# Moving the context's keys and values of a latent attention from the third phase of a two-layer kernel to its first, with the first phase's work put in a new order

## The chip, the cores and the metric

The kernel runs on 1 core of a Trainium2 chip. The metric is the device time of one execution in microseconds (us). A core has five engines with a queue of instructions each, worked through in order: TensorE (PE in the profile; PEld is its loading of weights), VectorE (DVE), ScalarE (ACT), GpSimd (POOL) and SyncE (SP), which here only starts DMAs. Engines wait for each other through semaphores. Matmul results land in PSUM, eight banks `Q[0]` to `Q[7]` of 128 x 512 float32.

## The reference

64 sequences of 128 tokens of width 256 go through two layers. Only what matters here is shown; `ctx_1024` is a second input, (64, 128, 256), that no step changes.

```python
x = x + L0_attn(layernorm(x), ...)            # state-space mixer: projection, convolution, decay matrices
x = x + L0_xattn(layernorm(x), ctx_1024, ctx_1024, mask, ...)   # cross attention on ctx_1024
x = x + L0_ffn(layernorm(x), ...)             # 16 experts, 2 per token, and a shared one
x = x + L1_attn(layernorm(x), ...)            # causal attention
x = x + L1_xattn(ctx_1024, layernorm(x), mask, ...)             # the latent attention
x = x + L1_ffn(layernorm(x), ...)             # ternary projection

# in L1_xattn(x=ctx_1024, latents=layernorm(x)):
x = layer_norm(x, ln_x_w, ln_x_b)             # of the context: depends on ctx_1024 alone
latents = layer_norm(latents, ln_l_w, ln_l_b)
kv = concatenate([x, latents], axis=1) @ Wkv  # 128 context rows, 128 latent rows
k, v = split(kv, 2, axis=-1)                  # 8 heads of 64
k = l2norm(k) * k_scale                       # per head: k / max(sqrt(sum k^2), eps)
```

The context's half of `k` and `v` does not depend on the stream `x`, so it can be computed at any time.

## The kernel before, in words

All 64 sequences are blocks of 128 tokens, one token on each partition. The program has three phases. Phase 1 does the mixer, the cross attention, the router and the shared expert; phase 2 the routed experts, tile by tile; phase 3 the causal attention, the latent attention and the last projection.

Phases 1 and 3 are software pipelines. The work of a block is cut into chains, and each chain into steps; a Python generator yields the name of each step and emits its instructions on one engine. In phase 1 the chains are M (first norm, time step, cumulative sums), V (projection, convolution), N (decay matrices and the mixer's output), Y (keys and values of the cross attention), X (cross attention) and F (router, shared expert). In phase 3 they are A (causal attention), C (the context's keys and values), K (latent queries, keys, values), L (latent attention) and T (output projection and ternary layer). `program(eng, engine, phase, stages)` gives each chain a lag in blocks, so that one round of the loop holds M and V of block n, N of block n-1, X of block n-2, F of block n-3. There are 64 blocks and a few rounds to fill and drain.

What stands behind what within a round is written out by hand: `ORDER[phase][engine]` is a list of tokens, the chain's letter and the step's name (`Ftop` is step `top` of chain F). `weave` walks the list. So each engine's queue is fixed, and a waiting instruction holds up all behind it. Names used below:

- `was(eng, name, b)` waits for the previous block's signal of that name, `done` for this block's.
- `Ncb0` to `Ncb3` (SP): the cumulative sums, written to memory by `Mco`, come back broadcast to all partitions, 512 KB for 8 heads each. `Nd0` to `Nd3` (POOL, L618) subtract from them, `Ng`, `Ne` (ACT, L1199, L1202) take the absolute value and the exponential, `Nm0` to `Nm2` (DVE, L847) and `Nm3` (POOL, L622) multiply by the masked product, `Nv0` to `Nv3` (PE) contract, `Ny0`, `Ny1` (DVE, L852) bring the result out, `Nyg` and `Nrms` (POOL) gate and scale it, `Npr` projects it, `Nx1` (DVE, L861) adds it to the stream.
- `Vcv` to `Vcv3` (DVE, L817 and L819): the convolution; `Vxs2` (L826) its gate; `VxsT` (PE) turns it; `Vxdt` (DVE, L836, L837) scales it; `Vz` (PE) is another projection into the same bank, so it waits for `Vxdt`; `Vtz` (ACT) and `Vgz` (DVE, L841) gate.
- `Ftop` (DVE, L893 to L905) picks two experts; `Fslot` their rows; `Fsc` (POOL, L646) scatters the rows to memory. `Mdt`, `Mab`, `Msp` make the time step; `Msp` on POOL is a chain of 13 small instructions (L594 to L610). `Xho` (DVE, L784, L785, L880) ends the cross attention with `x2`, from which the router's norm `Fln3` starts.
- Norms: moments on DVE, the root of the variance on POOL (`centre` or `rstd`), the scaling on ACT or DVE, the turn on PE, its copy on ACT.

Chain C in phase 3: load the context rows (`Cc`), norm them, turn them into `cT`, multiply by the keys' half of `Wkvl` (`Cla1`, in two halves `Cla1`, `Cla1h`), square (`Clq0` on ACT), sum per head (DVE), root (POOL, L682), scale (`Clu0`), turn (`ClT0`), copy into `klT`, then the values' half (`Cla3`, `Cla3h`) and copy into `Vl`. It uses bank `Q[3]` alone; K uses `Q[4]`. In phase 1 chain Y loads the same context rows, turns them on PE (`YcT`) and copies them (`cT` on ACT) before it multiplies.

## Time and profile before

| | |
|---|---|
| median of 3 runs | 4805.45 us (4796.27 to 4813.17) |
| the profiled execution | 4825.85 us, of it the span 4824.2 us |
| busy | PE 4196.8 us, DVE 3385.8, ACT 2902.8, POOL 2741.4 |
| phase 1 | 0 to about 2500 us |
| phase 2 | about 2500 to 2800 us |
| phase 3 | about 2800 to 4824 us |
| data moved | 304.09 MB, 63 GB/s over the span |

Read the three phases apart: PE is busy for 82% of phase 1 and for 99% of phase 3. The round of a phase is the first and the last start of an instruction that runs once a block, divided by 63.

### The profile page before, as it was taken

Reading aid. Unit: us, or ns where it says so; the run is one execution under the profiler, and the core shown is the slowest. Engines: PE = TensorE matmul, PEld = TensorE weight load, DVE = VectorE, ACT = ScalarE, POOL = GpSimd, SP = SyncE. Lnnn points to the kernel's source line nnn. Section 1 sums busy time; section 2 is a strip of 40 time slices with the busy share of each in tenths; the row PEclk is TensorE's granted clock in tenths of the full one; section 3 lists DMA queues with packets and bytes.
Section 4 is the critical chain, followed back from the end, with each engine's and each line's share of the span. In section 5 each row is a group of like instructions: output and inputs, shape, how many; then the busy total and the mean of one; then the engine's idle time right before and its main releaser. Section 6 shows DMA issues by size and latency. Waiting matters only on the chain. (4 is left out here: it accounts for less than half of the span.)

```text
span 4824.2 us, 120433 instructions
## 1 busy us (share of the span) xinstructions
PE 4196.8 (87%) x34006; PEld 3000.4 (62%) x34071; DVE 3385.8 (70%) x8668; ACT 2902.8 (60%) x7030; POOL 2741.4 (57%) x4093
## 2 busy tenths in 40 slices
PE   3888888888888888888869979999999999999998
PEld 2555555555555555555547756666666666666665
DVE  2776677666776677766745547877777777777776
ACT  2666666666666666666634436666666666666564
POOL 3666666666666666666622235555555555555554
PEclk8999999999999999999979989999999999999999
DMA  5222222222222222222214411111111111111110
GB/s 156 72 92 81 74 74 78 93 76 74 74 83 88 75 74 74 90 82 74 74 58 145 142 41 30 31 31 31 30 30 30 31 31 31 31 31 31 31 30 19
DMA packets 215885, 304.09 MB, mean 63 GB/s; under 512 B 56608, under 2 KB 167456, under 8 KB 215840
## 3 DMA queue, kind: packets, MB, share of 16 engines
q1 hardware_dynamic: 188864, 240.33, 16.2%
q0 software_dynamic: 19200, 52.45, 3.3%
q10 hardware_dynamic: 7776, 10.75, 0.7%
q8 instruction: 23, 0.38, 0.0%
q14 instruction: 22, 0.18, 0.0%
HBM read 239.19 MB, written 64.23 MB: 63 GB/s over the span
## 5 line engine op out<-in xcount | busy, mean ns | idle before, releaser
L1402 PE MATMUL Q<-ident,arena 128*128 128x128 f32 x4768 | 824.8, 298 | 141.0 <-ACT arena L1145 48.9
L1402 PEld LDWEIGHTS Q<-ident,arena 128*128 128x128 f32 x4768 | 570.3, 149 | 385.2 <-issue 135.8
L1397 PE MATMUL Q<-Wkvl,arena 128*128 128x512 f32 x1024 | 498.7, 599 | 0.0
L618 POOL TENSOR_TENSOR arena<-arena 128x1024 f32<-128x1024 f32 x256 | 479.6, 1890 | 6.7 <-DMA arena<-cum_rows 6.7
L682 POOL TENSOR_TENSOR l<-l,half_pow 128x8 f32<-128x8 f32 x192 | 318.8, 1661 | 230.4 <-DVE l L1025 228.8
L707 POOL TENSOR_TENSOR arena<-arena,part_of 128x512 f32<-128x512 f32 x256 | 264.1, 1043 | 188.6 <-DVE part_of L1063 187.7
L769 DVE TENSOR_REDUCE mx<-Q 128x4 f32<-128x512 f32 x512 | 343.8, 681 | 9.3 <-PE Q L1425 4.7
L1440 PE MATMUL Q<-arena 128*17 128x128 f32 x4096 | 243.2, 313 | 102.3 <-ACT arena L1162 102.2
L1431 PE MATMUL Q<-ident,arena 128*128 128x128 f32 x2048 | 300.0, 280 | 23.3 <-ACT arena L1162 18.4
L1431 PEld LDWEIGHTS Q<-ident,arena 128*128 128x128 f32 x2048 | 231.9, 141 | 132.3 <-issue 93.6
L1155 ACT ACTIVATE arena<-Q,mx 128x128 f32<-128x128 f32 x1024 | 282.6, 374 | 0.5 <-DVE mx L769 0.5
L1425 PE MATMUL Q<-arena 32*128 32x128 f32 x4096 | 281.9, 276 | 0.0
L1202 ACT ACTIVATE arena<-arena 128x1024 f32<-128x1024 f32 x256 | 268.6, 1049 | 0.1
L1199 ACT ACTIVATE arena<-arena 128x1024 f32<-128x1024 f32 x256 | 268.1, 1047 | 0.0
L1425 PEld LDWEIGHTS Q<-arena 32*128 32x128 f32 x4096 | 262.8, 189 | 3.2
L1361 ACT ACTIVATE arena<-Q,mxl 128x256 f32<-128x256 f32 x512 | 235.8, 473 | 46.2 <-DVE mxl L1058 38.9
L1497 PE MATMUL Q<-arena 128*16 128x128 f32 x4096 | 164.3, 278 | 107.6 <-DVE arena L847 98.1
L1440 PEld LDWEIGHTS Q<-arena 128*17 128x17 f32 x4096 | 146.4, 106 | 178.2 <-issue 163.8
L1162 ACT ACTIVATE arena<-Q 128x512 f32<-128x512 f32 x384 | 220.0, 589 | 56.6 <-PE Q L1431 55.8
L847 DVE TENSOR_TENSOR arena<-arena 128x1024 f32<-128x1024 f32 x192 | 233.2, 1242 | 2.9 <-ACT arena L1202 2.9
L1397 PEld LDWEIGHTS Q<-Wkvl,arena 128*128 128x128 f32 x1024 | 169.6, 190 | 103.8 <-issue 103.6
L819 DVE SCALAR_TENSOR_TENSOR arena<-arena,convw 128x128 f32<-128x128 f32 x768 | 225.8, 356 | 6.8
(312 smaller groups left out, 10634.8 us busy)
## 6 DMA issues: line engine op xcount, KB each, us to landing
arena<-cum_rows SPq DMA_DIRECT2D x256, 512.0 KB, 6.3
arena<-routed_rows SPq DMA_DIRECT2D x144, 128.0 KB, 2.1
expert_rows<-arena POOLq DMA_DIRECT2D x144, 128.0 KB, 2.0
arena<-in_x_dram SPq DMA_DIRECT2D x128, 128.0 KB, 5.1
arena<-in_ctx_dram SPq DMA_DIRECT2D x128, 128.0 KB
x_rows<-arena SPq DMA_DIRECT2D x128, 128.0 KB, 1.7
arena<-x_rows SPq DMA_DIRECT2D x128, 128.0 KB, 2.4
out_dram<-arena SPq DMA_DIRECT2D x64, 128.0 KB, 1.7
```

The lines of the kernel that those rows point to most:

```text
L618: tell(g.tensor_tensor(E8[j], E8[j], cums[:, 8 * j:8 * j + 8].unsqueeze(2).broadcast_to([P, 8, T]), ALU.subtract), "diff")
L682: link(pool, c, b, g.tensor_tensor(l2[:, k, :], l2[:, k, :], half_pow[:, :], ALU.pow), bare=True)
L707: tell(g.tensor_tensor(both, both, part_of[:, 2 * k:2 * k + 2].unsqueeze(2).broadcast_to([P, 2, 2 * T]), ALU.mult), "Pln")
L769: largest = v.tensor_reduce(mx[:, 4 * j:4 * j + 4], pj, AX.X, ALU.max, negate=True)
L1155: last = s_.activation(S[:, j, g, :], banks[j][:, g * T:(g + 1) * T], ACT.Exp, bias=mx[:, 4 * j + g:4 * j + g + 1])
L1199: tell(s_.activation(Ew[j], Ew[j], ACT.Abs), "gap")
L1202: tell(s_.activation(Ew[j], Ew[j], ACT.Exp, scale=-1.0), "E")
L1397: last = mm(out, lhs(c), rhs(c), start=c == 0, stop=c == n - 1)
L1402: last = nc.tensor.transpose(out[:, c * P:(c + 1) * P], src[:, c * P:(c + 1) * P], ident[:, :])
L1425: last = mm(banks[j][:, g * T:(g + 1) * T], QT[r, g, :], KT[r, g // 2, :], start=False, stop=g == NG - 1)
L1431: last = nc.tensor.transpose(bank[:, g * T:(g + 1) * T], S[:, j, g, :], ident[:, :])
L1440: last = mm(bank[32 * (h % 4):32 * (h % 4) + AW + 1, h // 4 * T:(h // 4 + 1) * T], V[:, h, :], PT[:, j, g, :], start=True, stop=True)
```

## The change

Chain C leaves phase 3 and joins phase 1 with the lag of chain X. Its keys and values are written to two new tensors in memory by a new chain S on SP one round later, and chain L of phase 3 loads them into the places where C had put them. C in phase 1 has two new tiles of 512 columns (`sqc`, `vlc`) which it uses again and again, and it uses bank `Q[2]` in turn with chain Y, where it had `Q[3]` to itself. Chain Y no longer turns the context: the host passes a second, transposed copy of `ctx_1024`, which SP loads straight into `ctxT`. `Wkvl` is loaded with the first weights. In phase 1 the norm of the context writes with a `tensor_scalar`. All ten lists of `ORDER` are new. Bank waits follow: `Yk` waits for the previous `Vl0`, `Clncn` for `v0c` and `k0c`; the filler matmuls of `cum` start after `dt_pre`.

The data path (shortened; the lists of `ORDER` are cut to those of PE):

```diff
 ORDER[1]
         "PE": """
-            YcT Yk Nv0 Fln3n Yv Xln2n Fr Mln1n Xq Vbc Mdt Frk Xs0 Fgu Fguh Vip1 Vip1h FhT Xs2 Fdn Mcum Nv1 Nv2 Xt0 Nv3 Xt1 Ny0 Xt2 VCB Ny1 Xt3 Xpv Xpv0 VxsT Xpv1
-            Xpv2 NyT Xpv3 Vz Vzh Npr Nprh XOT
+            Yk Yv Nv0 Fln3n Fr Nv1 Mln1n Nv2 Vbc Mdt Vip1 Xln2n Frk Vip1h Xq Nv3 Ny0 Clncn Xs0 Cla1 Cla1h Fgu Fguh Ny1 Mcum FhT Xs2 Fdn ClT0 NyT VCB Cla3 Npr Nprh
+            Xt0 VxsT Xt1 Xt2 Xt3 Xpv Vz Vzh Xpv0 Xpv1 Xpv2 Xpv3 Cla3h XOT
         """,
 ORDER[3]
         "PE": """
-            Two Twoh Aln4n Ls0 Kln6n Aq Clncn Kla0 Kla0h Aqv Ak Cla1 Ls2 TaT As0 Ttern KlT1 Cla1h Lt0 As3 Lt1 Kla2 At0 At1 Kla2h At2 At3 Apv Apv0 Apv1 Apv2 Apv3
-            Lt2 Lt3 AOT Lpv0 AoT ClT0 KlT2 Apr Lpv1 Cla3 Cla3h Kla4 Kla4h
+            Two Twoh Ls0 Kln6n Kla0 Aln4n Kla0h Aq Aqv Ak Ls2 TaT As0 KlT1 Ttern Kla2 Kla2h As3 Lt0 Lt1 At0 Lt2 At1 At2 At3 Apv Apv0 Apv1 Apv2 Apv3 Lt3 AOT Lpv0
+            AoT KlT2 Apr Lpv1 Kla4 Kla4h
         """,
...
+    kl_d = nc.dram_tensor("context_keys", (NB, P, KV), F32)
+    vl_d = nc.dram_tensor("context_values", (NB, P, KV), F32)
...
+        sqc, vlc = part(512), part(512)
+        xnc, cT = sqc[:, 0:D], cut(vlc[:, 0:D], DC)
...
             def Y(b):
                 yield "c"
-                was(sp, "ctxTps", b)
-                tell(sp.dma_start(ctx0, rows(ctx_d, b)), "ctx0_in", 16)
+                was(sp, "v0", b)
+                tell(sp.dma_start(ctxT, ctxt_d[bass.ds(b, 1)].rearrange("a (c p) t -> p (a c) t", p=P)), "ctxT_in", 16)
+
+            def C(b):
+                yield "c"
+                was(sp, "lnc_xn", b)
+                tell(sp.dma_start(ctx0, rows(ctx_d, b)), "ctx0_in", 16)
+
+            def S(b):
+                yield "k"
+                done(sp, "klT0", b)
+                tell(sp.dma_start(rows(kl_d, b), sqc), "kl_out", 16)
+                yield "v"
+                done(sp, "Vl0", b)
+                tell(sp.dma_start(rows(vl_d, b), vlc), "vl_out", 16)
...
             def L(b):
+                yield "k"
+                was(sp, "Sl", b, 4)
+                tell(sp.dma_start(klT[:, :, 0:T], cut(rows(kl_d, b), 4)), "kl_in", 16)
+                yield "v"
+                was(sp, "PVl", b)
+                tell(sp.dma_start(Vl[:, 0, :], rows(vl_d, b)), "vl_in", 16)
...
+            def C(b):
+                con = lambda c: cT[:, c, :]
+                yield "lncn"
+                done(pe, "v0c", b)
+                done(pe, "k0c", b)
+                lnT("lnc", xnc, Q[2], b)
+                yield "la1"
+                done(pe, "lnc_T", b)
+                last = yield from halves("la1", Q[2][:, :], con, lambda c: Wkvl[:, c, 0:KV])
+                tell(last, "la1")
+                yield "lT0"
+                done(pe, "kn0", b)
+                tell(transposes(Q[2], sqc, 4), "kT0")
+                yield "la3"
+                done(pe, "klT0", b)
+                last = yield from halves("la3", Q[2][:, :], con, lambda c: Wkvl[:, c, KV:2 * KV])
+                tell(last, "la3")
...
-            program(pe, "PE", 3, (("A", A, 0), ("C", C, 1), ("K", K, 1), ("L", L, 2), ("T", T_, 3)))
+            program(pe, "PE", 3, (("A", A, 0), ("K", K, 1), ("L", L, 2), ("T", T_, 3)))
```

Three places show how the order moved. The order gives one row for each form of instruction in a row; a float32 matmul is one here and two records in the trace.

On GpSimd, phase 1, from the last of the 13 steps of `Msp` to the first subtractions of the next round. Before, `Nm3` (L622) and the scatters come first, and three subtractions (L618 x3) open the round:

```order
L610 TENSOR_TENSOR arena<-arena,Aneg 128x32
L622 TENSOR_TENSOR arena<-arena 128x1024
L646 DMA routed_rows<-arena,meta 133248x256 x2
L625 TENSOR_TENSOR arena<-arena 128x512
L628 TENSOR_TENSOR ss<-ss,eps 128x1
L629 TENSOR_TENSOR ss<-ss,half_pow 128x1
L364 UNCONDITIONAL_BRANCH
L364 ISA
L125 ISA
L618 TENSOR_TENSOR arena<-arena 128x1024 x3
```

After the change the context's root (L672, L673) follows `Msp`, the scatters (L666) come last, and four subtractions (now L638) open the round:

```order
L630 TENSOR_TENSOR arena<-arena,Aneg 128x32
L672 TENSOR_TENSOR l<-l,half_pow 128x8
L673 TENSOR_SCALAR l<-l 128x8
L645 TENSOR_TENSOR arena<-arena 128x512
L648 TENSOR_TENSOR ss<-ss,eps 128x1
L649 TENSOR_TENSOR ss<-ss,half_pow 128x1
L666 DMA routed_rows<-arena,meta 133248x256 x2
L367 UNCONDITIONAL_BRANCH
L367 ISA
L127 ISA
L638 TENSOR_TENSOR arena<-arena 128x1024 x4
```

The step before the four subtractions moved: `Nm3` (now L642) runs ahead of `Msp`, and the fourth subtraction, which stood behind the norms, stands ahead of them.

On TensorE, the end of a round of phase 1. Before, `VxsT` (the first L1402 x4) is followed by the rest of the value product (L1440), `NyT`, and only then `Vz` (L1397 Win) and `Npr` (Wout); `XOT` ends the round:

```order
L1402 MATMUL Q<-ident,arena 128x128 x4
L1440 MATMUL Q<-arena 17x128 x8
L1402 MATMUL Q<-ident,arena 128x128 x4
L125 REGISTER_ALU
L1440 MATMUL Q<-arena 17x128 x4
L125 REGISTER_ALU
L1397 MATMUL Q<-Win,arena 128x512 x2
L1397 MATMUL Q<-Wout,arena 128x256 x4
L125 REGISTER_ALU
L1402 MATMUL Q<-ident,arena 128x128 x4
```

After the change `Vz` is followed by the whole value product (L1460) and the second half of `Cla3` (Wkvl); `Npr` stands before `VxsT`, outside this piece:

```order
L1451 MATMUL Q<-ident,arena 128x128 x4
L127 REGISTER_ALU x2
L1417 MATMUL Q<-Win,arena 128x512 x2
L1460 MATMUL Q<-arena 17x128 x12
L127 REGISTER_ALU
L1460 MATMUL Q<-arena 17x128 x4
L1417 MATMUL Q<-Wkvl,arena 128x512
L127 REGISTER_ALU
L1422 MATMUL Q<-ident,arena 128x128 x4
```

The value product and half of `Cla3` moved to between `Vz` and the end of the round.

On TensorE, phase 3, from the second product of scores' first part (the row of 256 columns, `Ls0`) on. Before, the latent rows are turned (`Kln6n`, the first L1402 x2), then comes `Aq` (Wq), then `Clncn`, then `Kla0` (Wql):

```order
L1744 MATMUL Q<-arena 128x256 x4
L130 ISA
L125 ISA
L1402 MATMUL Q<-ident,arena 128x128 x2
L125 ISA
L1390 MATMUL Q<-arena,Wq 128x128 x4
L130 REGISTER_ALU
L125 REGISTER_ALU
L1402 MATMUL Q<-ident,arena 128x128 x2
L125 REGISTER_ALU
L1397 MATMUL Q<-Wql,arena 128x512 x2
```

After the change `Kla0` stands directly behind `Kln6n`, whose result it waits for through ScalarE, and `Aln4n` and `Aq` stand behind it:

```order
L1761 MATMUL Q<-arena 128x256 x4
L132 ISA
L127 ISA
L1422 MATMUL Q<-ident,arena 128x128 x2
L127 REGISTER_ALU
L1417 MATMUL Q<-Wql,arena 128x512
L132 ISA
L127 REGISTER_ALU
L1422 MATMUL Q<-ident,arena 128x128 x2
L1417 MATMUL Q<-Wql,arena 128x512
L127 ISA
L1410 MATMUL Q<-arena,Wq 128x128 x4
```

The products with Wq and the turn of C no longer stand between the turn of the latent rows and their product.

## Rows read from the trace of the kernel before

**Rows 1.** Two stretches: PE, PEld, DVE, ACT, POOL busy, PEclk, DMA share, GB/s

```profile
1000.00:1500.00 500.00, 409.86 (x3538) 295.75 (x3551) 348.72 (x923) 324.22 (x700) 320.77 (x483) 0.94 0.24 79
...
3300.00:3800.00 500.00, 495.03 (x4001) 345.43 (x4000) 397.86 (x954) 312.79 (x832) 285.58 (x406) 1.00 0.11 30
```

**Rows 2.** Instructions that run once a block, phase 1 and 3: first, last start

```profile
L880 DVE TENSOR_TENSOR arena<-arena x64: 424/426/482, 144.4 to 2493.9; 128x256 f32<-128x256 f32 x64
...
L1018 DVE TENSOR_TENSOR arena<-Q,arena x64: 424/425/425, 2832.4 to 4761.0; 128x256 f32<-128x256 f32 x64
```

**Rows 3.** Chain that ended last, phase 3: start us, us, what

```profile
3310.57 0.86 PE Q L1397 x2
...
3315.34 1.46 PE Q L1402 x12
```

**Rows 4.** Order of time, phase 3, PE: turn of the latent rows, then `Aq`

```profile
3510.92 0.44 PE L1402 MATMUL Q<-ident,arena 128*128 128x128 f32 x2
3511.20 1.06 PE L1390 MATMUL Q<-arena,Wq 128*128 128x128 f32 x8
```

**Rows 5.** Order of time, phase 3, ACT: the copy of that turn

```profile
3511.40 0.81 ACT L1140 ACTIVATE arena<-Q,lnl 128x128 f32<-128x128 f32 x2 [1.37 <-PE Q L1402]
```

**Rows 6.** Order of time, phase 1, DVE; in brackets the idle time before

```profile
1156.45 0.43 DVE L880 TENSOR_TENSOR arena<-arena 128x256 f32<-128x256 f32 x1 [0.22 <-DVE arena L785]
...
1163.43 0.17 DVE L893 RECIPROCAL rt<-rt 128x1 f32<-128x1 f32 x1 [0.17 <-ACT rt L1257]
...
1172.04 2.41 DVE L847 TENSOR_TENSOR arena<-arena 128x1024 f32<-128x1024 f32 x2
...
1175.90 3.23 DVE L817 SCALAR_TENSOR_TENSOR arena<-arena,convw,convb 128x128 f32<-128x128 f32 x4
...
1183.41 0.69 DVE L826 SCALAR_TENSOR_TENSOR arena<-arena 128x512 f32<-128x512 f32 x1 [0.36 <-ACT arena L1190]
1184.02 0.42 DVE L852 TENSOR_TENSOR arena<-Q,arena 128x256 f32<-128x256 f32 x1
```

**Rows 7.** One line, 1000 to 1500 us: ns min/median/max

```profile
L817 DVE SCALAR_TENSOR_TENSOR arena<-arena,convw,convb x52: 334/340/2459, 1025.9 to 1479.4; 128x128 f32<-128x128 f32 x52
```

**Rows 8.** Order of time, phase 3, DVE: the norm's scaling, the sum per head

```profile
3511.36 0.47 DVE L762 SCALAR_TENSOR_TENSOR arena<-arena,mvC 128x256 f32<-128x256 f32 x1
...
3527.82 0.68 DVE L1025 TENSOR_REDUCE l<-arena 128x8 f32<-128x512 f32 x1
```

**Rows 9.** Order of time, phase 1, POOL

```profile
1157.85 0.19 POOL L582 TENSOR_TENSOR mvF<-mvF,eps 128x1 f32<-128x1 f32 x1 [0.17 <-DVE mvF L755]
...
1168.76 0.24 POOL L594 TENSOR_TENSOR arena<-arena 128x32 f32<-128x32 f32 x1 [4.59 <-DVE arena L804]
...
1176.31 2.41 POOL L622 TENSOR_TENSOR arena<-arena 128x1024 f32<-128x1024 f32 x1
...
1186.57 3.74 POOL L618 TENSOR_TENSOR arena<-arena 128x1024 f32<-128x1024 f32 x2
```

**Rows 10.** The page's groups: the root of the squared norms, busy and mean ns

```profile
L682 POOL TENSOR_TENSOR l<-l,half_pow 128x8 f32<-128x8 f32 x192 | 318.8, 1661 | 230.4 <-DVE l L1025 228.8
```

**Rows 11.** Order of time, phase 1, SP: write of the sums, then their loads

```profile
1177.84 0.35 SPq L437 DMA_DIRECT2D cum_rows<-arena  x1
...
1180.25 1.84 SPq L446 DMA_DIRECT2D arena<-cum_rows  x3
```

**Rows 12.** DMA issues, 1150 to 1190 us: KB each, median us to landing

```profile
arena<-cum_rows SPq DMA_DIRECT2D x4, 512.0 KB, 6.8
```

**Rows 13.** Order of time, first rounds, POOL: end of `Msp`, first subtractions

```profile
67.31 0.34 POOL L610 TENSOR_TENSOR arena<-arena,Aneg 128x32 f32<-128x32 f32 x1 [0.18 <-POOL arena L609]
74.32 5.61 POOL L618 TENSOR_TENSOR arena<-arena 128x1024 f32<-128x1024 f32 x3 [6.67 <-DMA arena<-cum_rows]
```

**Rows 14.** Two stretches, PE alone: busy, granted clock, DMA share, GB/s

```profile
1180.00:1190.00 10.00, 8.15 (x62) 0.83 0.80 279
2850.00:2875.00 25.00, 21.01 (x130) 0.93 0.10 28
```

**Rows 15.** The first 100 us, columns as in rows 1

```profile
0.00:100.00 100.00, 26.21 (x120) 19.17 (x126) 24.39 (x73) 16.73 (x30) 29.42 (x83) 0.86 0.55 162
```

188 lines of the change are left out of this document (84 added, 104 removed).

## The prediction

> **What bounds the kernel now.** I read first the busy time by stretch, since the phases have different limits. In phase 3 TensorE is busy for 495 of 500 us at full clock; in phase 1 for 410 of 500 at a clock of 0.94, and no other engine is over 70% there [rows 1]. Then the length of a round: 37.29 us in phase 1, from (2493.9 - 144.4) / 63, and 30.61 us in phase 3, from (4761.0 - 2832.4) / 63 [rows 2]. The chain of waits in phase 3 is nearly all TensorE, so there a microsecond of matmuls is a microsecond of time. In phase 1 no queue is full: a round is a ring of waits through all engines. I follow it on VectorE [rows 6]: `x2` of the oldest block is ready at 1156.88; the router's norm, turn, product and exponential take until `Ftop` at 1163.43 (6.55 us); from there VectorE works almost without a gap to `Vxs2` at 1183.41 (19.98 us); turn, scaling, projection and the end of the cross attention make the next `x2` (the rest, 37.29 - 26.53 = 10.76 us). The change is a trade: work off the full engine of phase 3, onto the ring of phase 1.
>
> **Phase 3.** Chain C has 8 records of 512 columns (0.86 us for two) and 6 turns (1.46 us for twelve) [rows 3]: 3.44 + 0.73 = 4.17 us a round. Without it TensorE has 30.61 - 4.17 = 26.44 us of work, the floor. C was also the filler behind which other chains waited. `Kla0` now stands directly behind `Kln6n`: from the start of the turn at 3510.92 to the end of ScalarE's copy at 3512.21 are 1.29 us, of which the turn itself takes 0.28 [rows 4, 5], so TensorE stands for 1.0 us. Everything behind `Kla0` waits too, `Aln4n` and `Aq` among it. Three more round trips through a copy lose a half of Wkvl or the 4 turns of `ClT0` as cover: `KlT1` to `Kla2`, the value product to `AOT`, `AoT` to `Apr`. Each costs between 0 and the 0.86 us of the cover lost; I take 0.3 each, since other work of A and L still stands between most of them, and 0.9 in all. The round becomes 26.44 + 1.0 + 0.9 = 28.3 us; the gain is 2.3 x 63 = 145 us. Bounds: 26.9 (the one wait alone, half hidden; -234 us) and 29.9 (three times the full 0.86; -45 us). VectorE, ScalarE and GpSimd only lose work, and the loads of keys and values (256 KB each) are issued a round ahead of use; hidden by it. If one of them came late, `Ls0` near the round's start would show it.
>
> **Phase 1, leg 1, `x2` to `Ftop`.** ScalarE now has an exponential (`Ne2`) and M's norm ahead of the router's, and VectorE has `Nm2` (half of 2.41 us) between `Fr` and `Ftop` [rows 6]. Between 0 and 1.2 us; I take 0.6, since part of it runs while the router's product is under way: 7.15 us.
>
> **Leg 2, VectorE from `Ftop` to `Vxs2`.** Of the 19.98 us, 0.36 are a wait, and the first step of the convolution took 3.23 us for four instructions whose median is 0.34 [rows 6, 7], so 1.87 us are a block: GpSimd's `Nm3` ran from 1176.31 to 1178.72 [rows 9], and one of the four took 2459 ns. Work is thus 17.75 us. `Nm1` and `Nm2` leave for leg 1 (-2.41); `Clncn` 0.47, the sum per head 0.68, the scaling of as many elements 0.68, and `Ny1` 0.42 come in (+2.25) [rows 6, 8]: 17.59 us. Blocks of the same kind are to be expected from what now stands side by side. `Nm3` runs ahead of `Msp`, beside `Fslot`, whose third instruction reads two SBUF operands: of its 1.9 us (half of 3.74, the same size) I take 1.1. The root `Clq0` (1.66 us [rows 10]) follows `Msp` while VectorE is at `Vcv1`: 1.6. With 0.3 beside the small steps and the old 0.36 this gives 3.4, between 0.4 and 5.5 (each block full, and a fourth for `Vxs2` against the first subtraction). Leg 2 is 21.0 us.
>
> The Trainium skill, "SBUF — State Buffer", section "SBUF: two separate sides", says why: VectorE with two SBUF inputs and a GpSimd instruction that reads SBUF take a shared pair of ports as an exclusive lock, and the loser stands until the other is through. The trace agrees (2459 ns against 340, beside a GpSimd instruction of 2.41 us). Were the ports a bandwidth that both share, the 3.0 us of blocks in leg 2 and the 0.5 below would not be there and the sum would be some 220 us lower.
>
> **Leg 3, `Vxs2` to `x2`.** `Npr` (8 records of 256 columns, half of 0.43 each, 1.72 us) and `NyT` (4 turns, 0.49) leave the stretch between `VxsT` and the end; `Cla3h` (0.86) enters it [rows 3]: 10.76 - 1.72 - 0.49 + 0.86 = 9.4 us. The last addition reads two SBUF operands beside GpSimd's subtractions of 1.87 us: 0 to 1.87, I take 0.5.
>
> The round is 7.15 + 21.0 + 9.4 + 0.5 = 38.05 us, 0.76 more: 0.76 x 63 = +48 us. The turn `YcT` and its copy are gone, but both lay beside waits, so that is worth nothing here. TensorE's own work would allow less: 30.8 us of records (409.86 of 500 us), and 4.17 more, less two turns. The moved SP steps wait for things long done, except that two writes and a second context load are between the sums' loads.
>
> **The ring through GpSimd.** A second ring has to fit. From the end of `Msp` to the write of the sums 1.53 us, to their first load 2.41, landing 6.8 [rows 9, 11, 12], four subtractions 7.48, the `x1r` addition about 0.7, then from the router's norm to `Msp` 10.91, and `Msp` 7.55 [rows 9]: 37.4 us, where before only three subtractions stood ahead (35.5, under the round). Leg 1's 0.6 and leg 2's 1.1 and 0.47 lie in it: 39.5. But in the first rounds the sums were ready 6.67 us after `Msp` [rows 13], not 10.7, so it is between 35.5 and 39.5; its middle, 37.5, supports 38.05 and no less.
>
> **The start.** `Wkvl`, 1.05 MB, is waited for before anything runs; at 162 GB/s [rows 15] that is up to 6.5 us, 0 if it lands beside ScalarE's loads. I take 4.
>
> **Sum.** 4825.85 - 145 + 48 + 4 = 4732.85 for the profiled execution. That one stands 20.40 us over the median of 4805.45, so I predict 4712 us.
>
> **Rivals.**
> *TensorE keeps its floor.* Both phases come out near the low bounds: phase 3 at 27.0, phase 1 at its old 37.29 or less, because the new order puts each wait behind work. For it: 18% of phase 1 is idle on TensorE. Against it: `Kla0`'s wait is written in the order. 4805 - 227 + 4 = 4582, and 4647 halfway between this and the forecast.
>
> *The clock.* In 1180 to 1190 the clock is 0.83, a third of the stretch at 1.2 instead of 2.4 GHz, 1.7 us lost where it is not covered; in 2850 to 2875, with TensorE busy 84%, it is 0.93; while it was busy 99% it stayed 1.00 [rows 1, 14]. With 28.3 us for 26.4 of work TensorE comes to stand in pieces of up to 1 us. If every second round loses 1.7 us, that is +54: 4766. The Trainium skill, "TensorE: Matmul & The Clock Gate", section "HAM oscillation — how this bites in real kernels", tells of kernels in which short waits between groups throttle the clock again and again; what phase 1 shows fits it, and for phase 3 it speaks against this change.
>
> *Slower: the ring through GpSimd decides.* One mechanism: the four subtractions wait for the sums' loads, which now share the queues with 512 KB of writes and a second context load (0.77 MB on 2.5). If a load lands in 8.6 us instead of 6.8, the ring is 39.5 + 1.8 = 41.3. It decides from a phase-1 round of 37.29 + 141 / 63 = 39.5 us on. Halfway over that, at 40.3, +190: 4805 - 145 + 190 + 4 = 4854. For it: the loads are on the ring now. Against it: the sums' loads still go out first.
>
> *The move gains nothing in phase 3.* K's chain runs from `x4` over three products and two roots back to the next `x4`; it could be the new bound near 30.6, since roots (1.66 us) and sums are long. Against it: in the trace it has slack, because it waited behind C. 4805 + 48 + 4 = 4857.
>
> **Chances.** Forecast 0.46 (its own range 4650 to 4760), floor 0.22, clock 0.14, GpSimd ring 0.12, no gain in phase 3 0.06. From them: faster by over 0.3% 0.46 + 0.22 + 0.10 = 0.78 (0.3%, 14 us, is about what a measurement of this kernel tells from none), within 0.3% 0.06 (some of the clock case, some of the ring), slower 0.16. Range 4598 to 4818: it holds the forecast, most of the floor case and the clock, and leaves out most of the two slower ones.
>
> **What would show it.** Right: phase 3's round 27.5 to 29 us, a wait of about 1 us on ScalarE's copy ahead of `Kla0`, TensorE at 93% there; phase 1's round 37.5 to 38.6, `Vcv1` with one instruction near 1.7 us. Wrong: a phase-1 round over 39.5 with GpSimd waiting for the sums' DMA ahead of its first subtraction; or a phase-1 round under 37; or a phase-3 clock under 0.98.

## The result and the profile after

| | before | after |
|---|---|---|
| median of 4 runs, us | 4808.87 (4796.27 to 4813.17) | 5232.69 (5210.92 to 5240.95) |
| ratio, 95% interval | | 1.0877 [1.0856, 1.0898] |
| span of the profiled execution, us | 4824.2 | 5228.4 |
| a round of phase 1, us | 37.29 | 40.96 |
| a round of phase 3, us | 30.61 | 33.10 |

The kernel became 8.8% slower; 4712 was predicted, and the range ended at 4818. (Ratios here and below leave out slow executions, those over 1.5% above the fastest of the same kernel; only e13 has any, two of five, and the longer of them is its profiled one.) Both phases lost: 3.67 us a round in phase 1 (+231 us over 63 rounds) and 2.49 in phase 3 (+157 us). The rounds come from these two lines of the trace after, which answer to [rows 2] and have the same columns:

```profile
L900 DVE TENSOR_TENSOR arena<-arena x64: 424/904/4387, 158.9 to 2739.2; 128x256 f32<-128x256 f32 x64
...
L1061 DVE TENSOR_TENSOR arena<-Q,arena x64: 424/425/426, 3078.9 to 5164.0; 128x256 f32<-128x256 f32 x64
```

The start costs 14.5 us more (158.9 against 144.4). With 231 and 157 that is 402 of the 404 us by which the span grew.

The two stretches after, in the columns of [rows 1]:

```profile
1000.00:1500.00 500.00, 433.30 (x3416) 305.17 (x3427) 351.67 (x921) 328.76 (x696) 324.41 (x496) 0.91 0.26 87
3300.00:3800.00 500.00, 450.11 (x3472) 305.08 (x3468) 330.07 (x798) 243.20 (x677) 231.81 (x318) 0.91 0.14 40
```

TensorE was to have 93% of phase 3 at full clock. It has 90% at 0.91. Its count of matmul records in 500 us fell from 4001 to 3472; a round has about 15 fewer, since chain C had 14, and the rest is that a round takes longer.

**Phase 3.** In order of time, SyncE starts the load of the context's values, the write of x4 and then the mask:

```profile
4001.92 0.34 SPq L533 DMA_DIRECT2D arena<-context_values  x1
4002.56 0.36 SPq L525 DMA_DIRECT2D x_rows<-arena  x1
4003.18 0.34 SPq L536 DMA_DIRECT2D mask1i<-in_mask_BxS_bk_dram  x1
```

and TensorE, with its idle time in brackets:

```profile
4001.81 1.98 PE L1417 MATMUL Q<-Wkvl,arena 128*128 128x512 f32 x4
...
4006.97 0.39 PE L1756 MATMUL Q<-mrow,onesb 1*128 1x512 bf16 x2 [1.45 <-DVE mrow L1078]
...
4009.68 1.13 PE L1417 MATMUL Q<-Wql,arena 128*128 128x512 f32 x2 [0.90 <-ACT arena L1164]
```

The second wait is the one predicted ahead of `Kla0` (1.0 us forecast, 0.90 here). The first, ahead of `Ls0`, was not: L1756 adds the mask, whose row VectorE makes (L1078) when its load lands, 3.4 us after it was issued. It is 1.7 us on average of the 15 rounds in 3300 to 3800, 1.45 here. The same place before, SyncE and then TensorE:

```profile
3504.57 0.36 SPq L511 DMA_DIRECT2D x_rows<-arena  x1
3505.21 0.33 SPq L516 DMA_DIRECT2D mask1i<-in_mask_BxS_bk_dram  x1
```

```profile
3503.96 3.70 PE L1397 MATMUL Q<-Wkvl,arena 128*128 128x512 f32 x8
...
3509.54 0.39 PE L1739 MATMUL Q<-mrow,onesb 1*128 1x512 bf16 x2
```

The mask stood behind the write of x4 before, too, and that write waits for GpSimd's copy of x4. From VectorE's addition that makes x4 (3503.23 before, 4001.08 after) to the mask's load are 1.98 us before and 2.10 after: hardly later. What changed is TensorE. Between the same addition and the matmul with the mask it had 6.3 us of work before; now it is ready after 4.4 us, since half of the eight Wkvl records were chain C's (3.70 against 1.98 us) and `Aln4n` moved behind. So C's matmuls had covered this round trip, from x4 over its copy, its write and the mask's load to `Ls0`. That is read from the two traces; no run puts work back in their place. The load also took somewhat longer (median 3.7 us to land, 3.1 before).

What follows the two waits costs about as much again, by the clock. Two stretches of 5 us (columns of [rows 1]):

```profile
4060.00:4065.00 5.00, 4.84 (x50) 3.42 (x47) 1.44 (x4) 1.77 (x4) 2.91 (x4) 1.00 0.38 105
4075.00:4080.00 5.00, 5.00 (x14) 2.89 (x13) 2.11 (x6) 1.70 (x6) 0.74 (x2) 0.50 0.00 0
```

TensorE is busy for all of the second one at 1.2 GHz, half of its full 2.4.

**Phase 1.** SyncE again, which answers to [rows 11]; L484 writes x2 (`Fo`), L450 loads the sums, L468 writes the context's keys:

```profile
1212.19 0.33 SPq L441 DMA_DIRECT2D cum_rows<-arena  x1
...
1214.76 0.33 SPq L484 DMA_DIRECT2D x_rows<-arena  x1
1215.83 1.31 SPq L450 DMA_DIRECT2D arena<-cum_rows  x2
...
1219.71 0.34 SPq L450 DMA_DIRECT2D arena<-cum_rows  x1
1220.34 0.35 SPq L468 DMA_DIRECT2D context_keys<-arena  x1
1220.88 0.34 SPq L450 DMA_DIRECT2D arena<-cum_rows  x1
```

GpSimd at the same place, which answers to [rows 9]:

```profile
1220.91 7.75 POOL L638 TENSOR_TENSOR arena<-arena 128x1024 f32<-128x1024 f32 x4 [3.44 <-DMA arena<-cum_rows]
1228.63 1.72 POOL L655 TENSOR_TENSOR arena<-arena,bv0b 128x256 f32<-128x256 f32 x1
...
1241.36 2.36 POOL L642 TENSOR_TENSOR arena<-arena 128x1024 f32<-128x1024 f32 x1 [4.64 <-ACT arena L1226]
```

From the write of the sums to their first load are 3.64 us where there were 2.41. `Fo` stood between them before, too (it ends SyncE's list in both kernels), but did not wait; now it waits 1.4 us a round for `xo` (total, times, longest, 1000 to 1500 us):

```profile
SPq L484 <- DVE arena L940: 16.8, 12, 1.4
```

The third load goes out 3.88 us behind the first and the fourth 5.05; before, three went out together and the fourth 4.10 us behind. GpSimd stands 3.44 us for the first load, then again (4.64 us) for the last exponential. Two of the signs that the prediction named for being wrong are there: a phase-1 round over 39.5 with GpSimd waiting for the sums' DMA, and a phase-3 clock under 0.98.

### The profile page after: what moved, and what is told of

Its sections match the earlier page's. It is cut to its first block, busy times and chain, and to the rows that moved or that the text cites. A ratio compares the mean times of both kernels' runs of the same rounds, so it can differ in the third digit from the quotient of the medians.

```text
span 5228.4 us, 120857 instructions
## 1 busy us (share of the span) xinstructions
PE 4464.7 (85%) x33878; PEld 3112.3 (60%) x33943; DVE 3391.6 (65%) x8668; ACT 2888.9 (55%) x6966; POOL 2760.9 (53%) x4093
## 4 chain that ended last, share of the span: by engine, by line
PE 49%; POOL 14%; DMA 11%; issue 11%; ACT 6%; SPq 5%; DVE 3%; POOLq 1%; DVEq 0%; ACTq 0%
PE Q L1410 11%; PE Q L1422 8%; PE Q L1417 8%; DMA arena<-cum_rows 6%; DMA mask1i<-in_mask_BxS_bk_dram 4%; PE Q L1445 3%; POOL arena L638 3%; PE Q L1761 3%; PE Q L1632 2%; PE Q L1517 2%; PE Q L1451 2%; POOL arena L642 2%; POOL arena L655 2%; PE Q L1460 2%; PE Q L1644 1%
## 5 line engine op out<-in xcount | busy, mean ns | idle before, releaser
L1422 PE MATMUL Q<-ident,arena 128*128 128x128 f32 x4640 | 810.6, 297 | 229.6 <-ACT arena L1169 177.9
L1422 PEld LDWEIGHTS Q<-ident,arena 128*128 128x128 f32 x4640 | 548.3, 148 | 572.0 <-issue 206.0
L638 POOL TENSOR_TENSOR arena<-arena 128x1024 f32<-128x1024 f32 x256 | 492.7, 1935 | 251.3 <-DMA arena<-cum_rows 247.4
L1417 PE MATMUL Q<-Wkvl,arena 128*128 128x512 f32 x1024 | 530.5, 631 | 32.2 <-ACT arena L1363 29.4
L672 POOL TENSOR_TENSOR l<-l,half_pow 128x8 f32<-128x8 f32 x192 | 331.4, 1726 | 366.0 <-DVE l L947 366.0
L642 POOL TENSOR_TENSOR arena<-arena 128x1024 f32<-128x1024 f32 x64 | 150.9, 2358 | 350.2 <-ACT arena L1226 350.2
L1517 PE MATMUL Q<-arena 128*16 128x128 f32 x4096 | 216.8, 346 | 126.4 <-DVE arena L867 104.3
L1410 PE MATMUL Q<-arena,Win 128*128 128x128 f32 x1536 | 293.3, 350 | 3.6 <-ACT arena L1161 0.5
L1451 PE MATMUL Q<-ident,arena 128*128 128x128 f32 x2048 | 281.7, 276 | 17.1 <-ACT arena L1186 16.0
L1417 PE MATMUL Q<-Wql,arena 128*128 128x512 f32 x256 | 237.8, 1030 | 57.4 <-ACT arena L1164 57.4
L1410 PEld LDWEIGHTS Q<-arena,Win 128*128 128x128 f32 x1536 | 253.4, 251 | 33.9 <-issue 25.8
L1161 ACT ACTIVATE arena<-Q 128x256 f32<-128x256 f32 x256 | 98.2, 384 | 314.5 <-PE Q L1422 314.4
```

Of the source, the lines that this page charges most:

```text
L638: tell(g.tensor_tensor(E8[j], E8[j], cums[:, 8 * j:8 * j + 8].unsqueeze(2).broadcast_to([P, 8, T]), ALU.subtract), "diff")
L672: link(pool, c, b, g.tensor_tensor(l2[:, k, :], l2[:, k, :], half_pow[:, :], ALU.pow), bare=True)
L1410: last = mm(out, lhs(c), rhs(c), start=c == 0, stop=c == n - 1)
L1417: last = mm(out, lhs(c), rhs(c), start=c == 0, stop=c == n - 1)
L1422: last = nc.tensor.transpose(out[:, c * P:(c + 1) * P], src[:, c * P:(c + 1) * P], ident[:, :])
L1451: last = nc.tensor.transpose(bank[:, g * T:(g + 1) * T], S[:, j, g, :], ident[:, :])
```

## The experiments

Rounds are read from the same two lines as above in each run's trace. Each run has the kernel before beside it on the same chip, at 4813 to 4831 us. e11, e13 and e14 are medians of 5 or 6 executions, the others one execution each. e7 and e11 have the same phase 3 and differ there by 0.29 us a round, so a difference of 0.3 us a round between two single runs is not told from none.

| run | us | phase 1 | phase 3 |
|---|---|---|---|
| before / after | 4808.87 / 5232.69 | 37.29 / 40.96 | 30.61 / 33.10 |
| e2_fill_pool | 5055.51 | 40.66 | 30.72 |
| e3_old3_fill1 | 5067.96 | 40.91 | 30.65 |
| e4_sp_both | 4879.01 | 39.16 | 29.46 |
| e5_sp_ne3_fill | 4867.90 | 39.20 | 29.29 |
| e6_no_context | 5037.91 | 41.92 | 29.19 |
| e7_sp_fillers | 4791.68 | 38.10 | 29.15 |
| e8_old_order1 | 5594.35 | 50.89 | 29.04 |
| e9_old_order1_sp | 5592.73 | 50.88 | 29.03 |
| e10_fln3_aln4 | 4961.39 | 40.81 | 29.15 |
| e11_more_fill | 4779.14 | 37.75 | 29.44 |
| e12_sp_loads_only | 4893.73 | 39.45 | 29.39 |
| e13_msp_early | 4930.02 | 40.63 | 29.30 |
| e14_m3_on_dve | 4685.03 | 36.55 | 29.22 |
| e15_no_context_good | 5028.05 | 41.85 | 29.21 |

**e2_fill_pool: the clock in phase 3.** Idle matmuls (`awake`, which nobody reads) ahead of the two waits of phase 3; in phase 1 GpSimd's `Nd3` later.

```diff
 yield "la0"
+awake(Q[3][:, :], 4)
 done(pe, "ln6_T", b)
 ...
 yield "s0"
+awake(Q[3][:, :], 7)
 done(pe, "kl_in", b, 16)
 ...
-Nd0 Nd1 Nd2 Nd3 Xx1r Fln3 Mln1 Xln2 Clnc Nm3
+Nd0 Nd1 Nd2 Xx1r Fln3 Mln1 Xln2 Clnc Nd3 Nm3
```

> Two edits read apart. Phase 3: seven filler matmuls ahead of the mask's wait and four ahead of Kla0 on TensorE, into a bank that nothing uses, so TensorE works where it stood; the waits themselves stay as long. Theory 'half clock after the waits costs the difference between the 30.5 us of a round at full clock and the mean of 33.1': clock 0.99 or more, round 30.4 to 31.0 us. Rival 'the waits alone cost it': round unchanged at 33.1. Phase 1: the fourth subtraction stands behind the three norms and the context's root on GpSimd instead of ahead of x1r. Theory 'GpSimd ring': the router's norm starts 1.9 us earlier, round 39.0 to 39.6. Rival: Nm3 is the later one (its exponential comes later), round 40.5 or longer.

Measured: phase 3 30.72 us, with this line for its stretch:

```profile
3300.00:3800.00 500.00, 484.39 (x3891) 324.88 (x3890) 355.77 (x863) 258.93 (x723) 249.07 (x344) 1.00 0.15 43
```

The clock is full and a round 2.38 us shorter. The idle matmuls take none of the two waits away, they occupy time in which TensorE stood, so I put all of this down to the clock: 150 of the 157 us lost in phase 3. The other edit gave 0.3 us a round, no more than two runs differ by.

**e3_old3_fill1: the order of phase 3, and the clock in phase 1.** Phase 3 in before's order without chain C's steps (SyncE as in after), and sixteen idle matmuls ahead of ln3's turn in phase 1.

```diff
-Two Twoh Ls0 Kln6n Kla0 Aln4n Kla0h Aq ...
+Two Twoh Aln4n Ls0 Kln6n Aq Kla0 Kla0h ...
 ...
-lnT("ln3", xnF, Q[7], b)
+lnT("ln3", xnF, Q[7], b, 16)
```

> Two edits read apart. Phase 3: the lists of the kernel before with the tokens of chain C taken out, on VectorE, ScalarE, GpSimd and TensorE; SP keeps the changed kernel's list. So Aq stands again between Kln6n and Kla0, and the mask is used later (Aln4n stands ahead of Ls0). Theory 'late mask and Kla0': both waits shrink, round 28.5 to 30.0 us. Rival 'any order loses the filler': round 31 or more, since C's matmuls covered the waits. Phase 1: sixteen filler matmuls ahead of the router's turn Fln3n, where TensorE stands 2.6 us. Theory 'GpSimd ring': TensorE's clock there is not on the ring, round 40.3 to 41.0. Rival 'clock': the half clock behind that wait costs up to 1.9 us, round 39.0 to 39.6.

Measured: phase 3 30.65 us, at a clock of 0.97, between the forecasts of the theory and of its rival. In this order the mask is not waited for (0.9 us in all in 500 us, where after has 26.0): `Aln4n` stands ahead of `Ls0`. Other waits came in its place, on VectorE's scaling of a norm (L778, 21.1 us in 16 times) and on the scaling of the keys (L948, 13.7 us in 17). So C's matmuls had covered more than one wait, and this order gains nothing over before either. In phase 1 the clock rose to 0.96 and the round stayed (40.91): there the clock was beside the ring, not on it.

**e4_sp_both: SyncE's order alone.**

```diff
 # phase 1, SyncE; Go is Fo as a chain of its own, one round later
-Ncb0 Ncb1 Mx Xm Yc Ncb2 Sk Ncb3 Cc Sv Fm Mco Nx Fo
+Ncb0 Ncb1 Ncb2 Ncb3 Mx Xm Yc Go Sk Cc Sv Fm Mco Nx
 # phase 3, SyncE
-Ax Lk Lv Kx Lm Tx To
+Ax Lm Lk Lv Kx Tx To
```

> SP's order alone, in both phases. Phase 1: the four loads of the sums open the round, and the write of the shared expert's sum (Fo), which waits for xo, comes behind them as a chain of its own one round later; in the changed kernel the trace's chain runs from xo over Fo to the loads, and three other loads stand ahead of the third. Theory 'SP holds up the sums': the third load goes out 3.3 us earlier, round 37.7 to 39.0 us instead of 40.96. Rival 'GpSimd's queue and the ports' (the late Ne3 ahead of Nm3, blocks): only part comes through, round 39.5 to 40.7. Phase 3: the mask load goes out ahead of the loads of keys and values and of the write of x4. Theory 'late mask': round at full clock 30.46 - 1.4 = 29.0, and with one wait left and some half clock 29.5 to 31.0. Rival 'clock alone, any wait ahead of Kla0 does it': over 32.

Measured: 4879.01 us. SyncE's two lists, with every other queue as in after, gave back 354 of the 424 us lost; against the run of before beside it (4826.63) 52 us remain. Phase 3 is 29.46 with no idle matmul in it, and once the mask is early the wait of 0.90 ahead of `Kla0` remains and the clock holds:

```profile
3600.00:4100.00 500.00, 468.81 (x3925) 325.03 (x3924) 374.89 (x905) 274.90 (x769) 260.79 (x358) 1.00 0.16 45
```

In phase 1 SyncE and GpSimd now read, in order of time:

```profile
1200.90 2.04 SPq L446 DMA_DIRECT2D arena<-cum_rows  x4
```

```profile
1205.09 7.50 POOL L636 TENSOR_TENSOR arena<-arena 128x1024 f32<-128x1024 f32 x4
```

The four subtractions start without a wait for the DMA. The round is 39.16, and its chain of waits is mostly TensorE, at a clock that drops in each round:

```profile
1216.00:1218.00 2.00, 0.63 (x16) 0.35 (x16) 1.70 (x6) 2.00 (x3) 1.68 (x6) 1.00 0.00 0
...
1222.00:1224.00 2.00, 2.00 (x16) 1.78 (x9) 1.31 (x8) 1.26 (x2) 0.00 (x0) 0.50 0.00 0
```

**e12_sp_loads_only: which part of SyncE's order.** As e4, but `Fo` stays at the end of the round, ahead of the loads.

```diff
-Ncb0 Ncb1 Mx Xm Yc Ncb2 Sk Ncb3 Cc Sv Fm Mco Nx Fo
+Ncb0 Ncb1 Ncb2 Ncb3 Mx Xm Yc Sk Cc Sv Fm Mco Nx Fo
```

> After with two edits of SyncE's order alone: mask first in phase 3, and in phase 1 the four loads of the sums first, in one piece; the write of x2 (Fo) stays at the end of the round, ahead of them, where after has it. No idle matmuls. Theory A (SyncE waits there for xo, and the third load stands behind it, so that the write is what decides): phase 1 stays at 40.4 or more. Theory B (the loads and stores put between the second and fourth load decide): phase 1 39.0 to 39.5, as with both. Phase 3 29.46 in either case.

Measured: 39.45 us. The steps put between the second and the fourth load cost 1.5 us a round; the write of x2 ahead of them at most 0.3 more, which one run each does not tell from none, although GpSimd still waits for the DMA as often (waits of 1000 to 1500 us: total, times, longest):

```profile
POOL arena L634 <- DMA arena<-cum_rows: 41.4, 15, 3.5
```

The 41 us of waits in this row (44.3 in after, 0.8 in e4) were thus worth at most 0.3 us a round; what gave 1.5 left them standing.

**e5_sp_ne3_fill.** e4, with `Ne3` right behind `Ng3` on ScalarE and four idle matmuls ahead of `Kla0`.

```diff
-... Ng3 Xln2 Vbc Yv Ne3 Xmr ...
+... Ng3 Ne3 Xln2 Vbc Yv Xmr ...
```

> As the kernel with both SP lists changed, and two more edits. Phase 1: ScalarE's fourth exponential Ne3 directly behind Ng3 instead of behind the copies Vbc and Yv that wait for TensorE. Theory 'Nm3 is late through Ne3': GpSimd's wait of 4.6 us ahead of Nm3 shrinks by 2 us, the round by 0.5 to 2 against the kernel without it. Rival: with the sums early Nm3 is off the ring and nothing moves (within 0.2 us). Phase 3: four fillers ahead of Kla0. Theory 'clock': with the mask early and this filler the clock is 0.99 or more and the round 28.4 to 29.3 us. Rival 'K's chain of roots is the bound': clock full, but round over 30.

Measured: phase 1 39.20, no change. In 1000 to 1500 us GpSimd's wait for `Ne3` fell from 52.4 to 31.1 us, and its wait for VectorE's `Msp` behind it grew from 15.6 to 38.8: the one wait took the other's place. Phase 3 29.29.

**e6_no_context: the moved work itself.**

```diff
-Ng3 ... Xq Clncn NYt1 Clq0 Fth Mcum FhT Nsq Xm0 Xm1 ClT0 NyT ...
+Ng3 ... Xq NYt1 Fth Mcum FhT Nsq Xm0 Xm1 NyT ...        # and so on four engines
```

> Leaves out, in phase 1, all of chain C's work on the four engines (the context's keys and values are zeros); its loads and both writes to memory stay, and so does the new order and SP's list. Theory 'the new order and SP's list cost, not the added work': round stays at 39.5 or more of 40.96. Rival 'the added work costs': round falls to 37.3 or less. Phase 3: the mask load early as in the two others, and Aln4n on VectorE ahead of Tlno and Lm0, no filler: round 29.5 to 31, as without it; below 29.3 would say that the turn of A's norm was a wait of its own.

Measured: phase 1 41.92 us, a microsecond longer than with the work. Without it the clock is lower, too (0.84 against 0.91), and GpSimd waits longer for the sums' loads (63.9 against 44.3 us in 500). So the run does not say what the work costs by itself; it says that the round does not fall when the work goes.

**e7_sp_fillers: the clock in phase 1, with SyncE mended.** e4, and

```diff
-awake(Q[3][:, :], 5)            # ahead of Nv0
+awake(Q[3][:, :], 9)
-lnT("ln3", xnF, Q[7], b)
+lnT("ln3", xnF, Q[7], b, 8)
+awake(Q[3][:, :], 4)            # phase 3, ahead of Kla0
```

> SyncE's steps as in the run with both new SyncE orders (phase 1: sums' four loads, then the inputs, then the write of x2 of the round before, then keys and values; phase 3: mask ahead of the 256 KB loads), and short idle matmuls of TensorE: in phase 1 nine in place of five ahead of the first product of Nv0, eight of 256 columns ahead of ln3's transposes; in phase 3 four ahead of the projection Kla0. Theory A (phase 1 is now TensorE's own: half clock after 2 us of short waits near Nv0 and Fln3n costs about 3 us of 39.16): phase 1 36 to 37 us, clock 0.98 or more in 1000 to 1500, phase 3 29.3; 4680 to 4740 us in all. Theory B (another engine's ring stands behind it, GpSimd through Nm3 and ACT's Ne3): phase 1 stays at 38.8 to 39.3 with clock near 1, 4860 us.

Measured: 38.10 us, clock 0.97. Here, unlike in e3, the idle matmuls shorten the round (by 1.06 us), since TensorE had come to set it; the forecast of 36 to 37 was too low. Half clock was still granted in some rounds (about 6 us from 1190 to 1197, none in the next round); by the mean of 0.97 that is 2.3 us a round.

**e8_old_order1 and e9_old_order1_sp: before's order of phase 1 with C put in.** On TensorE, for example:

```diff
-Yk Yv Nv0 Fln3n Fr Nv1 Mln1n Nv2 Vbc Mdt Vip1 Xln2n Frk ...
+Yk Nv0 Fln3n Yv Xln2n Fr Mln1n Xq Vbc Mdt Frk Clncn Xs0 Cla1 Cla1h Fgu ...
```

> Phase 1: before's order on GpSimd, VectorE, ScalarE, TensorE and SyncE, with the steps of chain C (context's keys and values) and of the stores S put in between; phase 3: after's engines, mask first on SyncE, four idle matmuls ahead of Kla0. Theory A (the new order of phase 1 is what costs, the added work itself little, as the run without C's work says that stayed at 41.92): phase 1 38 to 39.5 us, phase 3 29.3, 4830 us or less. Rival (C's work does not fit into any order at under 40): phase 1 40.5 or more, 4930 us.

> As the run with before's order in phase 1, but SyncE's steps in the order of the run with both new SyncE orders (x2's write one round later, behind all four loads of the sums). If SyncE's order helps with every order of the engines: 1 to 2 us a round under its neighbour, 4740 us. Rival: before's order asks for xa and xr late, so it makes no difference of over 0.3 us a round.

Measured: 50.9 us in both, over 11 us above e8's forecast and on the side of both rivals; SyncE's order makes no difference here. Where C's steps stand, VectorE waits for GpSimd's root and TensorE behind it. The page's group of e8 (busy, mean ns, idle before):

```profile
L948 DVE TENSOR_TENSOR arena<-Q,l 128x512 f32<-128x512 f32 x192 | 132.2, 688 | 524.8 <-POOL l L669 524.8
```

In before's order GpSimd does `Clq0` (the root that VectorE's `Clu0` needs) behind `Msp`, `Nm3` and `Fsc`. So the runs say that C needs places of its own in all queues, which the new order gives; they don't say what before's order with better places would cost.

**e10_fln3_aln4.** e7 with ScalarE's `Fln3 Fln3n` ahead of `Ne1`, and VectorE's `Aln4n` earlier in phase 3.

```diff
-Ng0 Ne0 Ng1 Ne1 Ng2 Fln3 Fln3n Ne2 ...
+Ng0 Ne0 Ng1 Fln3 Fln3n Ne1 Ng2 Ne2 ...
```

> As the run with SyncE's order and idle matmuls, and two steps earlier: ScalarE's Fln3 and Fln3n (ln3's normalised rows) ahead of Ne1 and Ng2 in phase 1, VectorE's Aln4n right behind Kln6n in phase 3. Theory: TensorE's wait for Fln3n (1.0 us a round) goes, but Ne1 (and with it the masks of the products) is 0.6 to 2.7 us later: phase 1 within 0.5 us of its neighbour; phase 3 29.19 to 29.0 instead of 29.3. Rival: Ne1 delays GpSimd's ring and phase 1 gets longer by 1 to 2 us.

Measured: 40.81 us, the rival's side and 0.7 beyond it. The exponentials are late: GpSimd's wait ahead of `Nm3` grew from 3.1 to 7.7 us a round. But the chain that ended last does not go through GpSimd; it goes from the exponential over VectorE's product to TensorE, whose clock fell from 0.97 to 0.92. `Aln4n` gave nothing (29.15 in both).

**e11_more_fill.** e7, with idle matmuls at three more waits.

```diff
+awake(Q[4][:, :], 2)            # ahead of Fr
+awake(Q[4][:, :], 1)            # ahead of Nv2
-lnT("ln1", xn0, Q[0], b)
+lnT("ln1", xn0, Q[0], b, 3)
```

> As the run with SyncE's orders and idle matmuls (38.10 us a round in phase 1 with half clock for some 6 us of it, 29.15 in phase 3), with idle matmuls at three more short waits of phase 1: two of 512 columns ahead of the router's product (wait 0.47 us), three of 256 columns ahead of ln1's transposes (0.25 to 0.27), one of 512 ahead of Nv2 (0.34). Theory (the waits of 1.1 us in all between 1187 and 1190 are what still drops the clock): clock of 1000 to 1500 over 0.99 and phase 1 35.3 to 36.5 us; 4640 to 4700 us. Rival (a wait nobody fills, ahead of the sums or the query, drops it all the same, or GpSimd's Nm3 stands next at 37.5 to 38): 4770 to 4800.

Measured: 4779.14 us (4772.52 to 4790.69, 6 runs) against 4813.48, ratio 0.9926 [0.9911, 0.9940]: 0.7% faster, the first that is shown to beat before (e7 stood 32 us under the one run beside it). The clock is full:

```profile
1000.00:1500.00 500.00, 471.91 (x3960) 325.81 (x3958) 381.21 (x1005) 355.56 (x757) 361.73 (x535) 1.00 0.28 94
```

but the round is 37.75, not 36: the next ring runs through GpSimd and VectorE. In order of time, GpSimd's `Nm3`, VectorE's `Clncn` (L959), then the last of `Msp` on VectorE and what GpSimd waits for. `Clncn` stands beside `Nm3` in every round, 2.42 us on average where it lasts 0.41 in after:

```profile
1187.10 2.37 POOL L640 TENSOR_TENSOR arena<-arena 128x1024 f32<-128x1024 f32 x1 [2.76 <-ACT arena L1224]
```

```profile
1187.04 2.58 DVE L959 TENSOR_SCALAR arena<-arena,mvC 128x256 f32<-128x256 f32 x1
...
1191.12 0.19 DVE L822 TENSOR_TENSOR arena<-arena 128x32 f32<-128x32 f32 x1
```

```profile
1191.39 0.28 POOL L612 TENSOR_TENSOR arena<-arena 128x32 f32<-128x32 f32 x1 [1.92 <-DVE arena L822]
```

**e13_msp_early: that ring, by order.**

```diff
 # VectorE
-Mdt Clncn Fslot Msp Vcv
+Mdt Msp Clncn Fslot Vcv
 # ScalarE
-Ne3 Xmr Xln2n NYt0 Mab Vxp
+Ne3 Mab Xmr Xln2n NYt0 Vxp
```

> As the run with more idle matmuls (37.75 us a round in phase 1 at clock 1.00), with three steps moved: VectorE's Msp (three small operations of the decay) ahead of Clncn and Fslot, ScalarE's Mab right behind Ne3, and in phase 3 VectorE's Aln4n right behind Kln6n. In the trace the ring of phase 1 goes Ne3, GpSimd's Nm3 (2.36 us), in whose time VectorE's L959 (Clncn, 128x256) lasts 2.58 us, then five small operations of Fslot, then Msp, for which GpSimd waits 1.9 us. Theory (that wait is in the ring): GpSimd starts its decay 1.5 to 1.9 us earlier, phase 1 35.9 to 36.6 us, 4680 to 4720 us. Rival (TensorE's own work, 35.4 of 37.75 busy, or the clock is next): 37.0 to 37.6, 4730 to 4770. Phase 3: 29.0 to 29.4.

Measured: 4882.25 to 4969.11 us in 5 executions, median 4930.02, against 4827.52; ratio 1.0124 [1.0104, 1.0144]. Phase 1 is 40.63 in the profiled execution, the longest; the shortest is 87 us shorter, by which its round would be 39.2 or more (an estimate), still over the 37.75 of e11. The theory fell. `Msp`'s first operation, of 128x32, took the blocked place and lasted 1.9 us, and what started earlier on GpSimd were the subtractions, which then met `Vxs2` (L844, 128x512, 0.69 us when free):

```profile
1149.75 8.42 DVE L844 SCALAR_TENSOR_TENSOR arena<-arena 128x512 f32<-128x512 f32 x1
```

```profile
1150.17 7.45 POOL L636 TENSOR_TENSOR arena<-arena 128x1024 f32<-128x1024 f32 x4
```

One operation of VectorE stood behind four of GpSimd's, though by the records it started 0.42 us before them (GpSimd was issuing a scatter at that moment, 0.96 us from 1149.18). It does not happen in each round: in 1000 to 1500 us the mean of L844 is 4.09 us (0.76 in e11), over all 64 rounds its median is 0.69. Nor does it happen only here: the longest in e11 is 8.30 us.

**e14_m3_on_dve: that ring, by taking the blocking operation away.** e11, with the fourth product on VectorE, ahead of `Clncn`.

```diff
 # GpSimd, chain N
-yield "m3"
-done(pool, "E", b, 4)
-done(pool, "cbm", b)
-tell(g.tensor_tensor(E8[3], E8[3], cbm..., ALU.mult), "M3")
 # VectorE, chain N
-for j in range(3):
+for j in range(4):
     done(dve, "E", b, j + 1)
-    tell(v.tensor_tensor(E8[j], E8[j], cbm..., ALU.mult), "M")
+    tell(v.tensor_tensor(E8[j], E8[j], cbm..., ALU.mult), "M" if j < 3 else "M3")
```

> As the run with more idle matmuls (37.75 us a round in phase 1), with the fourth product of the masked decays (Nm3, 128x1024, 2.36 us on GpSimd) done by VectorE like the other three (1.24 us each), between Mdt and Clncn. Theory (mutual blocking is in the ring: while GpSimd does Nm3, VectorE's Clncn lasts 2.42 us instead of 0.4): VectorE gains 2.0 and pays 1.24, the decay chain starts 0.7 to 1.2 us earlier: phase 1 36.4 to 37.2 us, 4690 to 4750 us. Rival (as when Msp was moved ahead: what starts earlier on GpSimd's side makes the subtractions meet VectorE's Vxs2, which is then blocked for up to 8 us): phase 1 39.5 or more, 4900.

Measured: **4685.03 us** (4683.76 to 4697.79, 5 runs) against 4827.13, ratio 0.9709 [0.9695, 0.9722]. Phase 1 is 36.55 us, as the theory said (36.4 to 37.2):

```profile
1000.00:1500.00 500.00, 480.97 (x4065) 336.64 (x4090) 378.01 (x1051) 368.26 (x790) 341.31 (x536) 1.00 0.30 99
```

`Clncn` lasts 0.41 us again, and the chain that ended last no longer goes through GpSimd. The edit also takes 2.36 us of work off GpSimd's queue, so the block's own share of the 1.2 us that the round lost against e11 is not separated. TensorE is busy 96% of phase 1, but some 64 of these 481 us are idle matmuls. In the profiled executions (4697.79 against 4825.85) the gain over before is 0.74 us a round in phase 1 (47 us) and 1.39 in phase 3 (88 us), less 6 us at the start. It is the gain of all edits together, the added idle matmuls among them, which the kernel before did not get.

**e15_no_context_good: the moved work once more.** e11 without chain C's work on the four engines (the edit of e6).

> As the run with more idle matmuls, leaving out the context's keys and values of the latent attention on the four engines of phase 1 (chain C; zeros are written and read back; its load, both writes and both reloads stay). Theory A (in this kernel the decay's ring GpSimd-VectorE-ScalarE decides and C's work is beside it; C's Clncn is only what stands in the blocked place): phase 1 36.8 to 37.7 us. Theory B (TensorE's own work decides: C's matmuls there, 5.1 us a round by the lines, are all paid): 33 to 35 us.

Measured: 41.85 us where e11 with the work has 37.75; both theories missed. Two things are longer without C. One is that VectorE gets to the convolution (L840) earlier, while GpSimd subtracts; this is its longest round:

```profile
1162.86 7.22 DVE L840 SCALAR_TENSOR_TENSOR arena<-arena,convw 128x128 f32<-128x128 f32 x8
```

```profile
1164.10 7.74 POOL L639 TENSOR_TENSOR arena<-arena 128x1024 f32<-128x1024 f32 x4 [1.28 <-DMA arena<-cum_rows]
```

and the means of the convolution and of its gate in 1000 to 1500 us (in e11 346 and 758 ns):

```profile
L840 DVE SCALAR_TENSOR_TENSOR arena<-arena,convw 128x128 f32<-128x128 f32 x144 | 65.6, 518 | 0.4
...
L847 DVE SCALAR_TENSOR_TENSOR arena<-arena 128x512 f32<-128x512 f32 x12 | 18.2, 1517 | 1.1
```

That is 2.1 us a round for the twelve pieces and 0.8 for the gate. The other is the clock, 0.91 where e11 has 1.00:

```profile
1000.00:1500.00 500.00, 407.76 (x3379) 295.95 (x3402) 343.05 (x839) 291.56 (x623) 281.13 (x432) 0.91 0.26 86
```

TensorE stands 2.2 us a round while GpSimd makes the time step, and the products behind that wait, which are on the chain, run at half clock: the cross attention's scores (16 records) last 1.71 us instead of 0.89, the next four records 2.02 instead of 1.06, together 1.8 us a round. The blocks and the clock add up to about the 4.1 us; no run separates them. What the work costs by itself can't be read from leaving it out. e14 shows only that phase 1 with it, the idle matmuls and the other edits can be shorter than before without it.

## Why the prediction was wrong, step by step

- **Phase 3, the wait ahead of `Kla0`: right.** 1.0 us forecast, 0.90 measured.
- **Phase 3, the list of lost covers and "hidden by it": the step that failed first.** The prediction named the places where C's matmuls had covered a round trip (`Kla0` and three more) and priced them at 1.9 us. One was not in the list: from x4 over its copy, its write and the mask's load to `Ls0`. It was put at nothing, since the prediction asked only whether the loads of keys and values came in time. TensorE waited 1.7 us a round for the mask, ahead of `Ls0`, the step that the prediction had named as the place where a late load would show.
- **Phase 3, the clock: a rival given 0.14, mis-sized.** It was put at 1.7 us each second round; it took 2.38 each round (e2). The wait ahead of `Kla0` alone does not bring it about: with the mask first and no idle matmul the clock is 1.00 (e4). Whether the mask's wait alone would is not tested. The Trainium skill, "TensorE: Matmul & The Clock Gate", section "HAM oscillation — how this bites in real kernels", told of a kernel whose waits between groups of matmuls bring the lower clock back in each of its steps. The trace agrees in kind (half clock behind the two waits of each round), though the waits there are for DMAs and longer than those here (1.7 and 0.90 us).
- **Phase 3, the size of the gain: nearly right once the mask is mended, its terms less so.** 28.3 us a round forecast, 29.0 to 29.5 in the runs e4 to e15. In e4 TensorE stands 0.90 us ahead of `Kla0`, 0.5 ahead of `Kla2` and 0.3 ahead of `Apr`, so the three lost covers cost 0.8 where 0.9 was forecast. What is off is the floor: TensorE is busy for 27.6 us of e4's round (468.81 of 500 us), not 26.44. How much of that is work and how much the modelled ends of matmuls ahead of a wait is not shown.
- **Phase 1, "the moved SP steps wait for things long done": the second step that failed.** `Fo` waits 1.4 us for `xo`, and the exception that the sentence makes, the steps between the sums' loads, was named and then priced at nothing. They cost 1.5 us a round (e12); the wait of `Fo` costs at most 0.3. The rival "the ring through GpSimd" was right on place and sign. Its mechanism was half right: a load landed in 5.1 us (median), less than the 6.8 of [rows 12], but the later ones were issued up to 5.05 us after the first.
- **Phase 1, the clock: not in the sum.** With SyncE mended the round is 39.16 where 38.05 was forecast, and TensorE at a clock of 0.89 is most of its chain; idle matmuls gave back 1.06 us (e7) and, with more of them, 0.35 (e11). The legs were added up from durations at before's clock, 0.94. (TensorE's own work comes to 30.6 us of records a round, not 30.8; nothing rests on it.)
- **Phase 1, blocks between VectorE and GpSimd: right in kind, not in place.** `Fslot`'s third instruction took 1.76 us on average (forecast 1.3: 0.2 and a block of 1.1), the x2 addition 0.90 (forecast 0.9). The block of 1.6 at `Vcv1` did not come (L837 and L839, longest 540 ns in 1000 to 1500). e13 and e15 show why adding them one by one was unsafe: a block depends on what meets, and each moved step shifts what meets.
- **Phase 1, the added work: its price stays open.** The sum had 0.76 us a round for it and the new order. e6 and e15 can't price it, as leaving it out moves the blocks and the clock; e14 shows only that an order exists in which phase 1 with it takes 36.55 us.
- **The start: 4 us forecast, 14.5 measured**, 6 in e14. The rest was not looked into.

Of the 424 us between the medians, SyncE's two lists account for 354 (e4). They mend in phase 3 what the lost cover brought about, and need not be its cause. Against before, e4 still has 1.87 us more in a round of phase 1 (118 us) and 9 at the start, and 1.15 less in a round of phase 3 (72 us). Of the 1.87, idle matmuls took 1.4 and e14's edit 1.2 more.

## What to carry to other kernels

When a change takes work off a full engine, list every round trip that this work had covered, also those through a DMA: here the mask's load, behind a write that waits for x4, stood no later than before, and what had filled the time was gone. Such a load can be started earlier (e4). When a change adds steps to a queue that only starts DMAs, list for each old step behind them who waits for it. Short waits of TensorE can cost about as much again in clock (here 2.4 us of clock beside 2.6 of waits a round), so take their cause away or fill them. Where VectorE and GpSimd both read SBUF, moving or removing work changes what collides: here taking the colliding operation off GpSimd (e14) gained, and shifting what stands beside it (e13) lost.

## What the runs showed of the hardware that was not expected

A block of VectorE need not end with the GpSimd instruction that it met. One VectorE operation of 0.69 us lasted 8.42 us while GpSimd ran four instructions of 1.9 us back to back (e13). In e15, beside the same four, no piece of the convolution lasted over 2.07 us. What decides between the two is not shown. An operation as small as 128x32, 0.19 us when free, is blocked like a large one (1.9 us on average in e13). The Trainium skill, "SBUF — State Buffer", section "SBUF: two separate sides", gives the port pair to whichever starts first "for the whole instruction"; the case of instructions in a row, seen here, it leaves open.

Leaving work out lengthened phase 1 by 4.1 us a round (e11 to e15), with every engine less busy and the granted clock down from 1.00 to 0.91.

The phase-3 round of the same phase-3 code differs between kernels that differ in phase 1 alone, 29.15 in e7 and 29.44 in e11: 18 us that no edit explains.
